# One masked multiply in place of four fused compare-and-multiply instructions in a graph network's scatter stage

## The reference

```
x_j = h[dst]                                        # gathered per edge
m = einsum('ei,ej,ijh->eh', x_j, edge_attr_8, W_msg) * norm
m = silu(m) @ W_msg_lin * norm_lin
agg = segment_sum(m, src, 12500)                    # summed by the edge's source node
u = silu(einsum('ni,nh,ihk->nk', h, agg, W_upd) * norm_u) @ W_upd_lin * norm_lin
x = x + h + u                                       # h: layer-normed x, relu
```

## Time and profile before

| | us |
|---|---|
| median of 3 runs | 7577.99 |
| lowest to highest | 7573.52 to 7580.85 |
| the profiled execution, its time | 7580.85 |
| its span in the profile | 7579.1 |
| the first layer, from the start to about | 4150 |
| the second layer's loop over groups, about | 4280 to 7390 |
| PE busy | 6892.4 (91%) |
| DVE busy | 6492.7 (86%) |
| ACT busy | 4377.7 (58%) |
| POOL busy | 5712.3 (75%) |

### The profile page before, as it was taken

How to read it: one execution, slowest core, us unless ns; L and a number is a source line. 1 busy time by engine, 2 the same in 40 slices (tenths; PEclk the granted TensorE clock), 3 DMA queues, 4 the chain that set the end, 5 groups by cost and what they waited for, 6 DMA issues and landing times. The chain is left out here.

```text
span 7579.1 us, 190087 instructions
## 1 busy us (share of the span) xinstructions
PE 6892.4 (91%) x52101; PEld 5979.1 (79%) x52101; DVE 6492.7 (86%) x16891; ACT 4377.7 (58%) x8232; POOL 5712.3 (75%) x4880
## 2 busy tenths in 40 slices
PE   6999999999999999999997699999999999999984
PEld 4777777777777777777776599999999999999981
DVE  6888888888888888888888899999999999999985
ACT  3444444444444444444443577777777777777760
POOL 5777777777777777777776388888888888888880
PEclk9999999999999999999999899999999999999997
DMA  2111111111111111111111454444555555545442
GB/s 53 20 20 20 19 20 20 20 20 20 20 20 20 19 20 20 20 20 20 20 20 33 99 73 73 72 72 71 73 74 71 73 72 72 73 72 74 72 57 39
DMA packets 699525, 333.83 MB, mean 44 GB/s; under 512 B 422354, under 2 KB 643920, under 8 KB 699498
## 3 DMA queue, kind: packets, MB, share of 16 engines
q0 software_dynamic: 336128, 66.50, 15.4%
q1 hardware_dynamic: 362188, 263.59, 13.8%
q10 hardware_dynamic: 1182, 3.44, 0.1%
HBM read 300.69 MB, written 32.35 MB: 44 GB/s over the span
## 5 line engine op out<-in xcount | busy, mean ns | idle before, releaser
L695 POOL DMA_INDIRECT xg<-gather_rows,idx x3232 | 3069.1, 950 | 998.7 <-issue 980.3
L1445 POOL DMA_INDIRECT sums<-total,row x1616 | 2617.9, 1620 | 535.5 <-issue 410.0
L805 PE MATMUL ps_w<-W2s,hT 128*128 128x256 f32 x12928 | 2977.4, 383 | 46.2 <-DVE prod L869 43.4
L805 PEld LDWEIGHTS ps_w<-W2s,hT 128*128 128x128 f32 x12928 | 2431.7, 190 | 562.1 <-DVE prod L869 201.0
L1416 PE MATMUL ps_wide<-hot_col,placed 128*128 128x392 f32 x12928 | 2437.4, 346 | 20.2 <-ACT hot_col L1358 11.4
L1416 PEld LDWEIGHTS ps_wide<-hot_col,placed 128*128 128x128 f32 x12928 | 2317.0, 196 | 51.4 <-issue 39.0
L869 DVE TENSOR_TENSOR prod<-ps_w,xg 128x512 f32<-128x512 f32 x1616 | 1079.6, 689 | 502.3 <-DMA xg<-gather_rows,idx 338.9
L734 ACT ACTIVATE hT<-ps_h,b1c 128x512 f32<-128x512 f32 x1616 | 1018.0, 680 | 312.9 <-PE ps_h L793 312.0
L1257 DVE SCALAR_TENSOR_TENSOR placed<-iota,src_r,halves 128x512 fp32r<-128x512 bf16 x1616 | 1103.1, 744 | 0.1
L1352 ACT ACTIVATE square<-iota_col,minus_col 128x784 bf16<-128x784 int16 x1212 | 1056.4, 934 | 17.0 <-PE ps_wide L1416 17.0
L876 DVE TENSOR_REDUCE msg<-prod 128x32 f32<-128x512 f32 x1616 | 1058.6, 676 | 0.0
(11 more groups left out here) (185 smaller groups left out, 4995.7 us busy)
## 6 DMA issues: line engine op xcount, KB each, us to landing
dst_row<-dst_rows SPq DMA_DIRECT2D x404, 256.0 KB
xg<-gather_rows,idx POOLq DMA_INDIRECT x3232, 2.4
src_row<-src_rows SPq DMA_DIRECT2D x404, 128.0 KB
q_win<-q_rows SPq DMA_DIRECT2D x404, 96.0 KB
ea<-in_edge_attr SPq DMA_DIRECT2D x404, 64.0 KB
sums<-total,row POOLq DMA_INDIRECT x1616, 3.1
e<-in_edge_attr SPq DMA_DIRECT2D x404, 32.0 KB
q_rows<-Q SPq DMA_DIRECT2D x13, 768.0 KB, 3.5
```

The costliest lines, as they stand in the source:

```text
L695: pool.indirect_dma_start(xg[r][:, t, :], None, k.rows, bass.IndirectOffsetOnAxis(ap=idx[r][:, t:t + 1], axis=0)).then_inc(xg_in[r][t], 16)
L805: last = pe.matmul(bank[:, w, :, :].rearrange("p i o -> p (i o)"), hT[half][:, j, col:col + P], k.W2[:, j, :], start=(j == 0), stop=(j == 1))
L1445: pool.indirect_dma_start(k.sums[t], bass.IndirectOffsetOnAxis(ap=row[s][:, t:t + 1], axis=0), total[s][:, t, :], None, compute_op=ALU.add ...
```

## The change

`place` wrote `placed` with one `scalar_tensor_tensor` per tile: (iota == remainder) * half, with the remainder `src_r` as a per-partition scalar. Now a `tensor_tensor` compares iota with the remainders of all four tiles and writes a mask of 4 x 16 values per partition, in float32, and one `tensor_tensor` multiplies the mask by the halves of all four tiles, both read with broadcast, into `placed`. Between the two VectorE waits for its own result on a new semaphore, `mask_ready`. The mask has one buffer.

```diff
+    mask_r = sb("mask_r", [P, WIDE, HI], f32)
...
                     need(v, q["wide_done"], g - 1)
                     v.wait_ge(q["half_lo"], g + 1)
-                    for w in range(WIDE):
-                        last = v.scalar_tensor_tensor(
-                            placed[s][:, w, :, :, :].rearrange("p r f a -> p r (f a)"),
-                            k.iota[:, 0:HI].unsqueeze(2).broadcast_to([P, HI, 2 * D]),
-                            src_r[:, bass.ds(g, 1), w],
-                            halves[s][:, w, :, :].bitcast(f32).rearrange("p f a -> p (f a)").unsqueeze(1)
-                            .broadcast_to([P, HI, 2 * D]), ALU.is_equal, ALU.mult)
-                    last.then_inc(q["place_ready"], 1)
+                    v.tensor_tensor(mask_r[:, :, :], k.iota[:, 0:HI].unsqueeze(1).broadcast_to([P, WIDE, HI]),
+                                    src_r[:, bass.ds(g, 1), :].rearrange("p g w -> p (g w)")
+                                    .unsqueeze(2).broadcast_to([P, WIDE, HI]), ALU.is_equal
+                                    ).then_inc(q["mask_ready"], 1)
+                    v.wait_ge(q["mask_ready"], g + 1)
+                    v.tensor_tensor(
+                        placed[s][:, :, :, :, :].rearrange("p w r f a -> p w r (f a)"),
+                        mask_r[:, :, :].unsqueeze(3).broadcast_to([P, WIDE, HI, 2 * D]),
+                        halves[s][:, :, :, :].bitcast(f32).rearrange("p w f a -> p w (f a)").unsqueeze(2)
+                        .broadcast_to([P, WIDE, HI, 2 * D]), ALU.mult).then_inc(q["place_ready"], 1)
```

More of the change, by code:

```diff
@@ L1124, in layer1 @@
              "summed total_ready rowf_ready row_ready scatters_begun "
-             "half_hi half_lo col_ready squared col_ready_act place_ready wide_done acc_added").split()
+             "half_hi half_lo mask_ready col_ready squared col_ready_act place_ready wide_done acc_added").split()
     q = {n: sem(n) for n in names}
```

## The result

The changed kernel took 7811.53 us (median of 4 runs, 7764.95 to 7941.41) against 7575.9. The ratio is 1.0268, with a 95% interval of 1.0224 to 1.0314; it is taken over the profiled execution and the runs without that of 7941.41, which had a mean granted clock of 0.971 where the others had 0.979 to 0.984. The profiled execution took 7768.33, 187 more than that of the kernel before (7580.85). Of the 23 executions on record with this result, 15 took 7760 to 7768 and eight 7788 to 7959. Run again later in five rounds the kernel took 7761.23 (7757.06 to 7789.32), ratio 1.0254 (1.0236 to 1.0272). The forecast was 7995: the sign and the mechanism were right. The forecast increase of 417 us was about twice the measured one (236 by the medians, 187 by the profiled executions).

The account below looks back on a forecast made before the run. GpSimd's back-to-back scatters were taken as the bound, 7.70 us a group. Holds by the multiply made it 8.73: 404 x (8.73-7.70) = +416 on 7577.99, say 7995; lowest and highest points 7748 and 8241, 8-in-10 range 7620 to 8260.

Parts of the forecast that it names:

- GpSimd is the bound: Stage that runs place: GpSimd issues scatters back to back, four at 1.925 us making the 7.70 us period of a group.
- the forecast floor of 7.49 a group: TensorE's wide matmuls: 7.49 us apart in a period where the scatter did not hold them.
- Rival C: VectorE becomes the bound, the broadcast multiply at half rate (4.3 us): 9.2 us per group, 8180; chance 3%.
- Steps 1 to 5: VectorE's place: compare 0.21, wait 0.04, multiply 2.29, so 2.54 against 2.73; the 0.19 us saved is worth nothing.
- Step 6: Scatters beside place: the multiply holds at least one per group to its end, then 1.42 us more; +416 us.
- Rival A: The multiply does not hold the scatters; TensorE's 7.49 sets the period: 85 us faster, 7493; chance 15%.
- The formula: Scatter loop, second of a group held: two periods = h + 13.7 us; 8.12 a period with h = 2.54.
- h: Where a scatter's hold ends after the start of place: 2.54 at the multiply's end, 3.08 if hot_col keeps it out.
- the four balance points: Possible periods of the scatter loop: second scatter held 8.12 or 8.39 us, first held 9.07 or 9.34.
- I take the mean, 8.73: Period per group, taken as the mean of four possible ones: 404 x (8.73-7.70) = +416 us.

Follow-up runs that it names:

- the first control: The kernel before with both ps_s buffers in one PSUM bank, sum_rows behind the next group's gather, same_source moved up: 8599 against 7576.
- the moved compare: The changed kernel with the compare moved ahead of low: 7755.92 with one multiply, 7742.21 with four multiplies of 512 elements.
- the swap: The changed kernel with columns ahead of place in VectorE's order: 8062.83, ratio 1.0645.
- 7535: The changed kernel with the multiply cut in four of 512 elements, the compare still inside place: 7535.42, ratio 0.9937.
- 7742: The changed kernel with the multiply cut in four of 512 elements and the compare moved ahead of low: 7742.21, ratio 1.0202.
- the two multiplies (7769): The changed kernel with the multiply cut in two of 1024 elements each: 7768.66.
- the first order: Both ps_s buffers in one PSUM bank, sum_rows and same_source moved, against the kernel before; with the old instructions and iota in PSUM: 8599.
- the order of 7813 us: The changed kernel, mask in SBUF, ps_s in one PSUM bank, sum_rows and same_source moved, total_out and rows_out ahead of squares: 7813, ratio 1.0317.

## Why the prediction was wrong in size and right in kind

*GpSimd is the bound (right).* With three scatters a group both kernels take 7494 to 7497, the forecast floor of 7.49 a group. Rival C, VectorE as the bound, is out.

*Steps 1 to 5, place's own length (right).* 0.21, 0.04 and 2.29 us: measured 0.216, 0.04 and 2.293. The 0.19 us that it saves VectorE is not in the time.

*Step 6, the hold (right).* The removed instructions and the multiply both read two tensors in SBUF; with the mask in PSUM the multiply's hold is gone and 238 us with it. Rival A is out. A scatter that starts inside the multiply waits for its end and needs 1.43 us more. One reading was loose: the scatter that starts at 5025.28 overlaps 0.64 us of the first instruction of `place`, not all of its 0.74.

*The formula (right).* Two periods = h + 13.7 gave 8.12 with h = 2.54; measured 8.06 between the places shown and 8.16 in the mean; with h = 2.29 it gave 8.00, measured 8.00 at the places shown and 8.07 in the mean without the ten long periods.

*The step that failed* was the last one: "I cannot tell which the loop settles in ... I take the mean, 8.73". Of the four balance points the loop sat on the lowest, second scatter held to the multiply's end. Two of the four stood on `hot_col` keeping the scatter out, taken over from the single stretch of the earlier trace rows. In the changed kernel it never happens: all 368 that start inside the multiply end 1.42 to 1.44 behind it, and the longest, 3.64, is what one caught at the very start of the multiply needs (2.29 less 0.08, plus 1.43). It does occur elsewhere: in the first control 284 scatters that start in a short instruction of `place` wait to the end of `hot_col`. The other two stood on the first scatter being caught. That happens (it is what the moved compare and the swap ran into), but in the changed kernel the first one mostly starts 0.1 to 0.6 us before the multiply (median 0.39, which is 0.14 before the compare) and passes, and only 4 first ones were caught in 368 groups; I had called it "only just ahead of the block" and then gave it half the weight. So the term was mis-sized: 1.03 us a group forecast, 0.46 measured. A balance that holds itself, with everything in it near a row of the kernel before (the earlier trace rows with h alone changed), should have been the forecast, and the others the range.

Two things stay open. Why a waiting scatter is let in at the end of one short instruction and passed over at the next was not settled. It separates the two kernels with four multiplies (7535, where no held one is passed over, and 7742) in what their traces show; how much of the 207 us it makes was not measured. It has next to no part in the two multiplies (7769), where 360 of 368 wait for the instruction they start in. And none of the runs from 7787 up was profiled; that the loop spent part of them on a longer balance is likely from the moved compare's trace, and not shown.

## What to carry to other kernels

Before fusing VectorE instructions, look at what starts on GpSimd while they run: four short ones can leave gaps that one long one does not, and 0.19 us saved on an engine with slack cost 0.46 on the engine that bounds. Where the mean of an issue lies above its median, line up the long ones against the other engine's instructions and see where they end; that finds the coupling before any change is made. And in a loop that has settled into step, work out each balance point and forecast the one that the present rows are nearest to, not their mean.

## What the runs showed of the hardware that was not expected

- For this multiply the hold belongs to the operands, not to the length. With one input in PSUM a 2.29 us `tensor_tensor` held none of 1173 scatters (maximum 1.569 us), and a `scalar_tensor_tensor` with iota in PSUM held none beyond 1.691 in the first order, though its pointer scalar stayed in SBUF.
- Two SBUF tensors are not the only way to a hold. `hotT`, a `tensor_scalar` over one SBUF tensor (128x1024 int16 to bf16, 0.48 us), held 119 scatters in the kernel with four multiplies (7535), each until 1.42 to 1.44 behind its end (1.61 to 1.80 long); `hot_col`, also a `tensor_scalar`, shows the same. What sets these apart was not tested.
- The Trainium skill ("SBUF — State Buffer", Who interferes with whom) says that a VectorE instruction with two SBUF inputs contends with a GpSimd instruction that reads SBUF; the runs with the mask in SBUF and in PSUM agree. It also tells of a probe in which `tensor_tensor` did not stall DMA, and infers that descriptor generation needs the write interface, which `tensor_tensor` leaves free; for the indirect scatters here a `tensor_tensor` does stall them (2.36 us against 1.55).
- The scatter is open to it only near its own start. One that starts 0.24 us ahead of the compare overlaps 1.06 us of the multiply and still lasts 1.55. One that starts together with the first of four short multiplies (5001.55) lasts 1.55 too. In the order of 7813 us the 23 scatters that start up to 0.03 us behind the multiply's start pass, and the earliest of the 362 held starts 0.06 behind it.
- Back-to-back short instructions do not always leave a gap: 2.81 us for a scatter beside four multiplies of 0.68. In the kernel before, 311 of the 314 scatters that start inside `place` and last over 1.6 us were let in at the end of the first instruction they met, in the first control 8 of 295.
